# Image attention: the exponentials of the 154 context keys turned by a DMA transpose, their value rows doubled

## The reference, cut to what matters

```
xn   = layer_norm(layer_norm(x));  cn = layer_norm(ctx)      # 512 and 154 rows
q    = xn @ Wq * 64**-0.5                                    # 512 x 64
k, v = concat(xn, cn) @ Wkv                                  # 666 x 64 each
out  = softmax(q @ k.T) @ v                                  # over 666 keys
x    = x + tanh(g) * concat_heads(out) @ Wo
```

## Time and profile before

| | |
|---|---|
| median of 3 runs | 1663.16 us (1662.12 to 1663.86) |
| the profiled execution's own time | 1667.16 us |
| its span | 1665.3 us |
| PE busy | 1445.0 us (87%) |
| PEld busy | 985.4 us (59%) |
| DVE busy | 1110.9 us (67%) |
| ACT busy | 780.5 us (47%) |
| POOL busy | 877.9 us (53%) |
| granted TensorE clock, mean | 0.937 of full speed |

### The profile page before, as it was taken

One profiled execution on the slowest core, in us unless ns is written; L12 is line 12 of the kernel. 1 busy time (PEld: TensorE's weight loads), 2 busy tenths in 40 slices (PEclk: granted clock), 3 DMA queues, 4 the chain that ended last, 5 costly groups with the idle time before them and its releaser, 6 DMA issues.

```text
span 1665.3 us, 36883 instructions
## 1 busy us (share of the span) xinstructions
PE 1445.0 (87%) x13680; PEld 985.4 (59%) x13849; DVE 1110.9 (67%) x2918; ACT 780.5 (47%) x1566; POOL 877.9 (53%) x1308
## 2 busy tenths in 40 slices
PE   5999999999999897977888889979977777789987
PEld 3777777777777775755566555534544344434545
DVE  5889788878777773544764667854446567487753
ACT  4777667767766661632233355554234434211111
POOL 5789889978776693363335653422033332153330
PEclk8999999999999999998899899999987979789998
DMA  7333232111221111250000000000000000000000
GB/s 279 103 90 86 86 97 50 49 44 45 61 49 44 52 51 57 58 182 1 1 1 1 9 9 1 2 1 1 1 1 1 0 1 1 1 1 1 7 7 14
DMA packets 35479, 64.31 MB, mean 39 GB/s; under 512 B 7535, under 2 KB 25042, under 8 KB 34147
## 3 DMA queue, kind: packets, MB, share of 16 engines
q1 hardware_dynamic: 33831, 59.83, 12.2%
q0 software_dynamic: 1472, 2.12, 0.4%
HBM read 30.64 MB, written 12.66 MB: 26 GB/s over the span
## 4 chain that ended last, share of the span: by engine, by line
PE 35%; DVE 10%; ACT 4%; POOL 3%; issue 2%; DVEq 0%; ACTq 0%; POOLq 0%
PE banks L520 9%; PE banks L2210 3%; PE banks L2196 2%; PE banks L3058 2%; PE banks L3001 1%; PE banks L2723 1%; PE banks L2717 1%; PE banks L2163 1%; PE banks L495 1%; DVE work L2293 1%; PE banks L2199 1%; PE banks L1763 1%; PE banks L305 1%; PE banks L2985 1%; PE banks L1687 1%
## 5 line engine op out<-in xcount | busy, mean ns | idle before, releaser
L1059 POOL TENSOR_TENSOR work<-work 128x512 bf16<-128x512 f32 (+1 forms) x512 | 358.7, 723 | 76.4 <-ACT work L952 75.5
L835 DVE TENSOR_REDUCE work<-banks 128x1 f32<-128x666 f32 x256 | 216.4, 846 | 64.9 <-PE banks L752 62.2
L959 ACT ACTIVATE work<-banks,work 128x666 f32<-128x666 f32 x256 | 208.1, 813 | 30.3 <-DVE work L835 23.3
L952 ACT ACTIVATE work<-banks 128x512 f32<-128x512 f32 x256 | 152.8, 597 | 146.0 <-PE banks L763 145.7
L460 POOL TENSOR_TENSOR norm_room<-norm_room,minus_half 128x4 f32<-128x4 f32 (+1 forms) x56 | 53.1, 949 | 294.7 <-DVE norm_room L435 170.0
L763 PE MATMUL banks<-const,work 128*128 128x128 f32 x1024 | 159.2, 278 | 15.5 <-ACT work L952 12.3
L752 PE MATMUL banks<-work 128*128 128x154 bf16 (+1 forms) x898 | 160.4, 295 | 9.7 <-DVE work L909 1.6
L520 PE MATMUL banks<-work,weights_b 128*128 128x512 bf16 (+1 forms) x830 | 150.1, 337 | 13.6 <-ACT work L1348 7.0
L752 PEld LDWEIGHTS banks<-work 128*128 128x128 bf16 x1024 | 96.0, 98 | 80.6 <-DMA work<-work 2.8
L2293 DVE TENSOR_REDUCE work<-banks 128x2 f32<-128x308 f32 x192 | 87.0, 472 | 82.0 <-PE banks L2163 56.2
L791 PE MATMUL banks<-work 128*128 128x65 bf16 (+1 forms) x3840 | 136.6, 192 | 3.0 <-POOL work L1059 1.8
(11 more groups left out here) (463 smaller groups left out, 3294.7 us busy)
## 6 DMA issues: line engine op xcount, KB each, us to landing
work<-work SPq DMA_DIRECT2D x128, 166.5 KB, 2.8
sorted<-in_pads SPq DMA_DIRECT2D x10, 838.5 KB
weights_b<-in_weights SPq DMA_DIRECT2D x1, 4120.0 KB, 13.4
work<-scratch SPq DMA_DIRECT2D x64, 64.0 KB, 1.9
weights_b<-in_weights SPq DMA_DIRECT2D x1, 2824.0 KB, 12.3
weights_a<-in_weights SPq DMA_DIRECT2D x1, 2056.0 KB
weights_a<-in_weights SPq DMA_DIRECT2D x1, 2050.0 KB, 9.9
work<-work SPq DMA_DIRECT2D x32, 64.0 KB, 1.9
```

The costliest lines, as they stand in the source:

```text
L835: ve.tensor_reduce(self.neg_max[i % 4], self.slot[i % 2][:, 0:KEYS0], AX_X, ALU.max, negate=True).then_inc(self.mark("max"))
L952: ac.activation(self.probs_t[u % 2][:, h, 0:4, j * P:(j + 1) * P], self.bank_a.rearrange("p (t n) -> p t n", t=4), ACT.Copy).then_inc(self ...
L959: ac.activation(self.probs[i % 3], self.slot[i % 2][:, 0:KEYS0], ACT.Exp, bias=self.neg_max[i % 4]).then_inc(self.mark("exp"))
L1059: po.tensor_tensor(parts[:, :, :, 0], exact, parts[:, :, :, 1], ALU.subtract).then_inc(self.mark(event, i - 3))
```

## The change

The exponentials of the 154 context keys no longer go through PE. POOL splits them in place, in the exponential's own buffer (which grows to 512 + 192 words, the last 38 of them zero, and of which there are now 4). Each word is then two bf16 values, the low and the high part of one key. SP issues one DMA transpose per sub-block, of 128 x 384 bf16 values, to one of 8 buffers of 128 x 3 x 128. Its rows are low and high parts in turn, so the value rows of the context keys are written twice, to even and odd partitions, by six DMAs a group from a buffer `v_rows`. PE weighs each sub-block with 4 tiles of 3 part products as before, and 3 tiles (64 keys each) of 2: both parts of the exponentials by the values' high part, then by their low part. L772, L775, L797 and L843, L850, L851, the second L1059, L1065 and the layout of the last 32 columns go. The two transposes of the finished heads (L770) stay, on bank 5 alone. Exponentials i now wait until the transpose of sub-block i-4 has landed. SP's program runs over steps: query parts of the next group at i % 8 = 1, key parts at 5, the doubled values at 6, and behind them in each step the transpose of sub-block i-1. The weights for the next stage are issued after the first group's doubled values.

The diff, cut to its core:

```
@@ -565,18 +568,21 @@
...
-        self.probs = [self.place(KEYS0) for _ in range(3)]
+        self.v_rows = self.place(2, 2, 2 * VALUE, dt=BF16).rearrange("p t s (h d) -> p t s h d", h=2)
+        self.probs = [self.place(SEQ + WORDS0 * HALF_KEYS) for _ in range(4)]
-        self.probs_t = [self.place(2, KT0 - 1, 2 * P) for _ in range(2)]
-        self.rest, self.rest_t = ([self.place(P) for _ in range(2)] for _ in range(2))
-        self.ctx_last = self.place(2, P + 32, dt=BF16)
+        self.probs_t = [self.place(2, QT, 2 * P) for _ in range(2)]
+        self.words_t = [self.place(WORDS0, P, dt=BF16) for _ in range(TURNS)]
...
@@ -752,62 +756,61 @@
...
-        if sub < SUBS:
-            m = pe.transpose(ps[:, 0:P], prob[:, 4 * P:5 * P], self.eye)
-        if rest is not None:
-            pe.wait_ge(*self.at("gathered", 4 * rest + 3))
-            m = pe.transpose(ps[:, P:2 * P], self.rest[rest % 2], self.eye)
...
+            pe.wait_ge(*self.values_in(n))
...
-            for t in range(KT0 - 1):
-                for which, (of_values, of_probs, width) in enumerate(orders):
-                    pe.matmul(self.out_heads[:, 2 * j + h, 0:width], parts[:, h, t, j * P:(j + 1) * P, of_probs], v[:, t, of_values, h, 0:width],
...
-        if h == 1:
-            pe.wait_ge(*self.at("low_c", u))
-            rest = self.halves(self.rest_t[u % 2])
-            for which, (of_values, of_probs, _) in enumerate(orders):
-                m = pe.matmul(self.out_bank[:, 0:4 * VALUE], rest[:, :, of_probs], v[:, KT0 - 1:KT0 + 1, of_values, :, :].rearrange("p j h d -> p j (h d)"),
-                              start=False, stop=which == 2, skip_group_check=True)
-            m.then_inc(self.mark("weighed"))
+            pe.wait_ge(*self.turned_in(sub))
+            for t in range(WORDS0):
+                for of_values, width in ((0, D0 + 1), (1, D0)):
+                    m = pe.matmul(out[:, 0:width], self.words_t[sub % TURNS][:, t, :], v[:, QT + t, of_values, h, 0:width],
+                                  start=False, stop=(h, j, t, of_values) == (1, 1, WORDS0 - 1, 1), skip_group_check=True)
+        m.then_inc(self.mark("weighed"))
@@ -835,28 +838,13 @@
...
-                ve.tensor_copy(self.probs_t[u % 2][:, h, 4, j * P:(j + 1) * P], self.bank_b[:, 0:P]).then_inc(self.mark("kept_b", i - 2))
...
-                ve.wait_ge(*self.at("turned_b", i))
-                ve.wait_ge(*self.own("ve", ve.tensor_copy(whole, self.bank_b[:, P:2 * P])))
-                ve.tensor_tensor(self.halves(whole)[:, :, 0], self.bank_b[:, P:2 * P], self.halves(whole)[:, :, 1],
-                                 ALU.subtract).then_inc(self.mark("low_c", u))
...
@@ -947,16 +931,16 @@
...
-                if i >= 3:
-                    ac.wait_ge(*self.at("turned_b", i - 1))
-                    ac.wait_ge(*self.at("gathered", i - 3))
+                if i >= 4:
+                    ac.wait_ge(*self.at("turned_a", i - 3))
+                    ac.wait_ge(*self.turned_in(i - 4))
                 ac.wait_ge(*self.at("max", i + 1))
-                ac.activation(self.probs[i % 3], self.slot[i % 2][:, 0:KEYS0], ACT.Exp, bias=self.neg_max[i % 4]).then_inc(self.mark("exp"))
+                ac.activation(self.probs[i % 4][:, 0:KEYS0], self.slot[i % 2][:, 0:KEYS0], ACT.Exp, bias=self.neg_max[i % 4]).then_inc(self.mark("exp"))
@@ -1051,35 +1033,18 @@
...
-                u, _, _, _, h, j = self.image_sub(i - 1)
-                if (h, j) == (0, 0) and u >= 2:
-                    po.wait_ge(*self.at("turned_b", 4 * u - 1))
+                whole = self.probs[(i - 1) % 4][:, SEQ:KEYS0]
                 po.wait_ge(*self.at("exp", i))
-                po.tensor_copy(self.rest[u % 2][:, 32 * (2 * j + h):32 * (2 * j + h + 1)], self.probs[(i - 1) % 3][:, KEYS0 - 32:]).then_inc(self.mark("gathered", i - 1))
+                po.tensor_tensor(self.halves(whole)[:, :, 0], whole, self.halves(whole)[:, :, 1], ALU.subtract).then_inc(self.mark("low_c", i - 1))
             if i == 32:
                 po.wait_ge(*self.at("dma_weights1", 16))
@@ -1101,22 +1066,48 @@
...
+        for which in range(3):
+            self.image_heads_sp(sp, 0, which)
+        self.load_weights(sp, 1)
+        for i in self.image_steps():
+            n = (i - 1) // 8 + 1
+            if i % 8 in (1, 5, 6) and n < GROUPS0:
+                self.image_heads_sp(sp, n, (1, 5, 6).index(i % 8))
+                if i % 8 == 5 and 2 <= n < 2 + PAD_PARTS:
+                    self.pads_sp(sp, n - 2)
+            if 1 <= i < SUBS + 1:
+                sub = i - 1
+                if sub >= TURNS:
+                    sp.wait_ge(*self.at("weighed", (sub - TURNS) // 2 + 1))
+                sp.wait_ge(*self.at("low_c", sub))
+                words = self.probs[sub % 4][:, SEQ:].bitcast(BF16)
+                sp.dma_start_transpose(self.words_t[sub % TURNS], words).then_inc(self.mark(f"dma_turn{sub % TURNS}", n=16), 16)
+
+    def image_heads_sp(self, sp, n, which):
...
+        else:
+            sp.wait_ge(*self.at("v_low", 3 * n + 2))
+            if n >= 3:
+                sp.wait_ge(*self.at("weighed", 2 * (2 * n - 4)))
+            v = self.v[n % 3].rearrange("p t s h d -> p t (s h d)")
+            rows = self.v_rows.rearrange("p t s h d -> p t (s h d)")
+            for word in (0, 1):
+                for h, own in ((0, top), (1, bottom)):
+                    sp.dma_start(v[word::2, QT + h, :], rows[own, 0, :]).then_inc(self.mark("dma_values", n=16), 16)
+                sp.dma_start(v[word:2 * CTX_REST:2, QT + WORDS0 - 1, :], rows[0:CTX_REST, 1, :]).then_inc(self.mark("dma_values", n=16), 16)
```

More of the change, by code:

```diff
@@ L686, in image_pe @@
                 self.image_weigh_pe(pe, u, h)
-            if 2 <= i < SUBS + 2 or self.rest_due(i) is not None or self.mix_due(i) is not None:
-                self.image_turn_pe(pe, i)
+            if 2 <= i < SUBS + 2:
+                self.image_turn_pe(pe, i - 2)
+            if self.mix_due(i) is not None:
+                self.image_mix_pe(pe, self.mix_due(i))
             for what, b, _ in self.image_chores(i):
@@ L753, in image_scores_pe, with image_turn_pe, image_mix_pe, turned_in @@
         m.then_inc(self.mark("scores"))
[L755 to L776 removed]
+    def image_turn_pe(self, pe, sub):
+        pe.wait_ge(*self.at("exp", sub + 1))
+        ps = self.bank(pe, 4, "kept_a", sub)
+        for t in range(QT):
+            m = pe.transpose(ps[:, t * P:(t + 1) * P], self.probs[sub % 4][:, t * P:(t + 1) * P], self.eye)
+        m.then_inc(self.mark("turned_a"))
+    def image_mix_pe(self, pe, u):
+        ps = self.bank(pe, 5, "mixed", u + 1)
+        pe.wait_ge(*self.at("divided", u + 1))
+        for j in (0, 1):
+            m = pe.transpose(ps[:, j * P:(j + 1) * P], self.divided[:, 2 * j:2 * j + 2, :].rearrange("p h d -> p (h d)"), self.eye)
+        m.then_inc(self.mark("mix_turned"))
+    def turned_in(self, sub):
+        return self.at(f"dma_turn{sub % TURNS}", 16 * (sub // TURNS + 1))
+    def values_in(self, n):
+        return self.at("dma_values", 96 * (n + 1))
     def image_weigh_pe(self, pe, u, h):
@@ L895, in value_pieces @@
     def value_pieces(self):
-        return [(KT0 - 2, slice(0, CTX - 32), slice(2 * P, 3 * P))] + [(KT0 - 1 + j, slice(64 * j, 64 * j + 64), slice(3 * P, 4 * P)) for j in (0, 1)]
-    def rest_due(self, i):
-        t = i - 2
-        return t // 4 - 1 if t % 4 == 1 and 1 <= t // 4 <= UNITS else None
+        return [(slice(0, P), 0, slice(2 * P, 3 * P)), (slice(0, CTX_REST), 1, slice(3 * P, 4 * P))]
     def image_lows_ve(self, ve, n, part):
@@ L1103, in image_sp @@
         self.loads(sp)
+        for which in range(3):
[15 more added lines that the diff above has]
+    def image_heads_sp(self, sp, n, which):
         top, bottom = slice(0, D0), slice(D0, 2 * D0)
-        for n in range(GROUPS0):
-            q, k, low = self.q[n % 2], self.k[n % 2], self.q_part
+        q, k, low = self.q[n % 2], self.k[n % 2], self.q_part
+        if which == 0:
             sp.wait_ge(*self.at("q_low", n + 1))
```

132 lines of the change are left out of this document (46 added, 86 removed).

## The result

The changed kernel takes 1764.34 us (median of 4 runs, 1763.72 to 1765.09), the kernel before on the same chip 1663.43: a ratio of 1.0608, 95% interval 1.0590 to 1.0627. It is slower by 101 us, where 24 us less were forecast. The profiled execution spans 1762.2 us.

What follows compares the result with a forecast made beforehand. PE's instruction stream was taken as the bound (94% busy). From 1667.2 us, -30 (PE), -3 (bank 5), +1 (new path), +8.5 (start) gave 1643.7, less 4.0 for the median: 1639.7, rounded 1640; own range 1626 to 1651, overall 1626 to 1717.

Steps and rivals of the forecast that it cites:

- PE gives 33.7 us, nine tenths of them show: PE's stream in the image stage: 0.53 us less a unit, 64 times; 30 us expected to show, bounds 25 and 34.
- bank 5's waits go: PE's waits for L851 vanish because bank 5 no longer carries the gathered tile: 3 us, bounds 0 to 7.
- POOL, DVE, ACT: Work of these engines in the image stage: POOL 42 us less, DVE 111, ACT one small copy a group; counted at nothing.
- The new path: Exponentials waiting for transposes issued in order on SP behind query, key and value moves: put at 1 us lost.
- x: SP's time to issue one DMA transpose: taken as 0.6 us, possibly 1.4 to 1.8.
- y: Landing time of a DMA transpose: taken as 2.8 us.
- 2x + y below 4.4: Two transpose issues plus a landing after key and value moves must fit 4.4 us; expected 4.0, holding by little.
- rival 2: Transposes go one behind the other on the rings, 4.3 us a sub-block: 525 us more, about 2165; chance 0.11.
- The rate: SP's issues and waits per group, 7.6 us plus eight transpose issues: 12.4 us of 18 expected.
- rival 1: SP's queue becomes the bound: at 1.6 us per transpose issue 77 us above forecast, 1717 us; chance 0.26.
- The start: Start of the image stage: first query move queues behind the weights' load, delaying exponentials 4; 8.5 us lost, bounds 4 to 12.
- Rival 3: PE's gain hidden behind scores-to-copy chain; half of 33.7 us stays, 12 lost at start, 1658 us; chance 0.14.

Runs made afterwards that it cites:

- e_noturn: Changed kernel without any DMA transposes: PE weighs zero tiles in their place, exponentials wait for POOL's split alone; 1639.27 us.
- e_noval: Changed kernel without the six moves a group that double the value rows, context values zero in the weighing; 1666.56 us.
- e_pieces: Changed kernel with the weights' load cut into 16 pieces on SP's own queue, one every third step from step 10; 1761.64 us.
- b_turns: Kernel before with one DMA transpose a sub-block, read by nobody, in SP's queue and SP's program in steps; its stage ends 12 us later.
- v_width: Changed kernel with one transposing DMA of six blocks for each two sub-blocks, value moves and padding kept; 1761.58 us, ratio 1.0618.
- e_load: Changed kernel with the 4120 KB of weights issued once by ACT at step 1 instead of in SP's queue; 1752.19 us.
- e_block1: Changed kernel with only one of the three 128-column blocks transposed, same count of transposes; 1746.26 us, ratio 1.0561.
- v_all: Changed kernel with values doubled by PE, weights and padding on ACT's queue, one six-block transpose for two sub-blocks; 1699.03 us.
- v_dblp: Changed kernel with values doubled by PE, weights in 16 pieces on SP's queue, one transpose a sub-block; 1682.31 us, ratio 1.0129.
- v_last: Changed kernel with values doubled by PE, 16 weight pieces and padding on SP's queue, one six-block transpose for two sub-blocks; 1681.15 us, ratio 1.0124.
- v_thinpair: Changed kernel with values doubled by PE, 16 weight and 26 padding pieces on SP's queue, one six-block transpose for two sub-blocks; 1711.05 us, ratio 1.0346.
- e_spread: Changed kernel with weights in 16 pieces and padding in 26 pieces for 10, on ACT's queue; 1788.08 us.
- v_spread: Changed kernel with values doubled by PE, weights and padding in pieces on ACT's queue, one transpose a sub-block; 1699.99 us.
- v_thin: Changed kernel with values doubled by PE, 16 weight pieces and 26 padding pieces for 10 on SP's queue, single transposes; 1698.95 us, ratio 1.0267.
- b_spread: Kernel before with weights and padding in pieces on ACT's queue; 1655.96 us, ratio 1.0007.

## Why the prediction was wrong

**PE's part.** Right in kind, too large. The steps "PE gives 33.7 us, nine tenths of them show" (30) and "bank 5's waits go" (3) gave 22.6 us in e_noturn, which has both. Two readings were off. Rows 2 have PE late at bank 4 in 60 and 112 of 247 steps, so in nearly every second step and not in one out of four or five. And 17.9 us is not the shortest group: the next one after it, 139.52 to 156.91, takes 17.4, and the exponentials give 17.3 to 17.7 for the short groups further on. Those of e_noturn take 17.27, where the prediction had 17.9 - 1.05 = 16.9; nearly all of the gain is in the longer groups. Part of what PE saved went into waits at bank 4 (60 to 620 us, before and then e_noturn):

```profile
PE banks L763 <- ACT work L952: 10.3, 57, 0.6
...
PE banks L764 <- ACT work L935: 31.6, 113, 0.8
```

The weight loads' late issue there rises as well, from 30.9 to 50.4 us. PE is still the busiest engine, at 539 of 583 us; why the short groups stop at 17.27 was not tested.

**POOL, DVE, ACT.** Held: 0.451 us for 0.446 at the split, and all three less busy.

**The new path.** This is the step that failed: the cost of the new path in SP's queue, put at 1 us besides the start, measured at 120 by sub-block 255 (733.86 for e_noturn's 613.43). Two of its terms were too small. It put x = 0.6, from key moves that take 0.60; x is 1.2. It priced the six value moves at the cheapest plain row, 0.46 each or 2.76 us; they take 4.0 by their medians (four of 0.588, two of 0.832) and 4.55 in the group shown. The landing, y = 2.8, is 2.4.

The condition, 2x + y below 4.4 after the key moves, holds a slip of its own: y is counted from the start of the issue (46.07 to 48.62 above, and rival 2 reads rows 9 so too), so the last x is in it already. Without the slip it asks for x + y below 4.4, and 1.2 + 2.4 = 3.6 would have passed. With the value moves at 4.0 the bound is 3.2 and with 4.55 it is 2.6, so it fails in every group by 0.4 to 1.0 us. So by this sum x alone did not break it, the two terms together did, and e_noval and e_noturn show the same: either of them taken out brings back groups of 17.3 us. The rate has the same story. With 7.6 + 8x = 17.2 of 18 us x = 1.2 would have passed; with every measured term (0.58 + 0.59 + 0.85 of waiting + 0.46 + 2.4 + 4.0 + 9.6) it is 18.5 us, and 19.6 with some 0.05 us between one issue and the next, against 17.3 for PE's short groups. The other waits make it 21.2, where 12.4 were expected. So rival 1 happened, at a smaller x than it asked for (its break point was 1.3), because the rest of its sum was too small. Its price at x = 1.6 was 77 us more than forecast; it came to 125.

What I hold for shown: SP's in-order queue, with transposes and value moves in it, sets the pace. It waits for others in 76 of 660 us only; a fifth buffer moves the wait to the keys; sixteen small issues more cost what they take (9.9 us for 9.1, e_pieces); the six moves less give 94 us back. The price of a transpose is one per instruction (1.18 us for one block, 1.21 for three, 1.23 for six), and its bytes cost nothing by themselves in a steady group (b_turns, within 0.1 us of the kernel before in nearly every group). Not shown: how the loss divides between the rate of the queue and the order in it, since v_width, with 5 us less of issues a group, lost it to order and latency instead.

**The start.** 8.5 us expected, 11.6 measured; exponentials 4 at 48.62 for the sum's 47.0. The stall is there, behind the load, but not because of the queue's order: e_load has the same 12.5 us from the move's issue to its landing. SP waited to 45.57 for the move, not 43.1, in good part because the dearer value moves put the load at 31.18 and not 29.5. From there to exponentials 4 it took 3.05 us and not 3.9: x = 1.2 was hidden in the landing, by the slip above.

**The rings.** Rival 2 fell: transposes one behind the other would have landed later and later, and they land in 2.4 us by the median and 4.3 at most. One block and three blocks take 1.18 and 1.21 us of the issuing queue here (e_block1, after) and six take 1.23 (v_all), and the medians to landing are 2.3, 2.4 and 2.8 us, so three blocks do not cost three times as much. The 1.4 us for each block, one behind the other, was its author's estimate from a move of 64 KB, and no run shows it. What the prediction held against it is in the trace of before: the key moves, issued four in a row, land in 2.4 to 3.1 us, 2.8 by the median (L1115). The transposes resemble plain moves in their landing (2.4 us for 98 KB, beside 2.2 for moves of 64 KB and 3.0 for 166.5 KB) and not in their issue, 1.2 beside 0.6.

**Rival 3** is not what happened, though both its parts are there: 11.6 of its 12 us were lost at the start, and of the 33.7 us that it halves e_noturn shows two thirds.

No version of the change with the whole computation beats the kernel before. The nearest are v_dblp and v_last at 1.013 and 1.012.

## What to carry to other kernels

Before work goes from an engine to DMAs, add up the issuing queue for one period: each instruction at the dearest row that resembles it, the waits between them too, in order. Here 21 small issues needed more than the 18 us of a group, on an engine that shows no busy time. Look also from where a landing is counted, from the start of the issue or its end. An operation that is not in the trace is worth one run by itself before its price decides a forecast: x between 0.6 and 1.8 held most of the question, and the value moves the rest.

When a queue is full, take instructions out from between those that are awaited; merging these into fewer and larger ones delayed each here, and gave nothing in the three pairs of runs that differ by this alone (v_width 1.0618 for 1.0608, v_last 1.0124 for 1.0129, v_thinpair 1.0346 for 1.0267).

## What the runs showed of the hardware

- A transposing DMA takes 1.2 us to issue for one, three or six blocks of 128 columns (medians 1.182, 1.206, 1.232 us), twice a plain move of queries or keys (0.46 to 0.60; the value moves take 0.59 and 0.83), and lands 2.4 us after its issue begins in the changed kernel (median; 2.3 for one block, 2.8 for six in v_width). In the other runs with three blocks the median is 2.4 to 3.2 us and the longest 6.4 to 8.4.
- A load of 4120 KB keeps a small move from landing for about 12 us, whichever engine's queue it is in: the load is issued at 31.18 and 31.50 us and the move at 33.12 and 32.09, which SP sees landed at 45.57 and 44.55, about when the load itself lands (14.2 and 14.3 us after its issue).
- With padding loads on ACT's queue, single issues on SP are stretched, of transposes to 4.8 to 5.0 us (e_spread, v_spread, v_all) and of plain moves to 3.2 and 3.8 (e_spread), while the medians stay; with the load of 4120 KB alone there the longest transposing issue is 2.4 us (e_load), with no load there 2.5 (after). v_thin, with all its loads on SP's own queue, has one transposing issue of 4.1 us, so a second queue is not the only way to it. Why stays open.
- Beside awaited transposes a padding load on the same queue costs 1.9 us a group at 322.5 KB and 2.9 at 838.5 KB (v_thin and v_dblp, estimates). In the kernel before, padding of 322.5 KB on ACT's queue cost nothing (b_spread, 1.0007). Why stays open as well.
- TensorE's granted clock was 0.72 of full speed from 30 to 37 us, 0.66 from 37 to 48.6 us, where PE is busy 1.4 of 11.6 us, and 0.74 to 60 us; before, it was 0.89 from 30 to 37 us and 1.00 from then on. Over the window of the earlier trace rows it is 0.96 for 1.00. The lower clock is not what slows the stage: from 350 to 500 us the clock is 1.00, and the groups there still take 20 to 24 us, where most took 17.3 to 19.1 before.
